# Blocks 1 to 7 of the first GEMM as seven half-size products, with a new mixing of the tiles

## The chip, the cores and the metric

One core of a Trainium2 chip runs the whole program. The metric is the device time in microseconds; the median of three runs stands for a kernel.

## What is computed

x is 4 x 1024 x 1024 (batch, time, channels), fside has the same shape, W1 is 4096 x 1024, W2 is 1024 x 4096. A two-sided decaying average over time mixes the tokens, then a feed-forward layer is added to x. Cut to what matters:

```python
def reference(x, fside, cond, w, u, W1, W2):
    r, k, v, time_emb = x, fside, fside, cond
    tf = sigmoid(sum(time_emb))
    decay = exp(-exp(w)) * (0.5 + 0.5 * tf)
    ek = exp(minimum(k, 30)); ekv = ek * v
    # nf, df: running sums of ekv, ek forward in time, each step times decay
    # nb, db: the same backward in time
    euk = exp(minimum(u + k, 30))
    num = nf + nb - ekv + euk * v
    den = df + db - ek + euk
    mixed = sigmoid(r) * (num / maximum(den, 1e-8)) * (0.8 + 0.2 * tf)
    h = einsum('bsd,fd->bsf', mixed, W1)
    a = gelu(clip(round(h / 0.1)) * 0.1)
    return x + einsum('bsf,df->bsd', a, W2)
```

The entries of W1 and W2 are 0 or a sign times a power of two from 1 to 1/16, so they are exact in float16.

## The kernel before

The work is cut into eight blocks: four batches times two halves of the time axis, 512 tokens each. Channels lie on the partitions, tokens on the free axis. A block has two parts on TensorE: the hidden stage (first GEMM, `hidden`, L378; for the first two steps of block 0 `first_hidden`, L364) and the output stage (`output`, L393). Both use float16 operands and split each activation in a high and a low half, so that each weight tile of 128x128 meets two matmuls of 512 columns. That makes 8 channel tiles x 32 feature tiles x 2 = 512 matmuls per stage and block. Each result of the hidden stage goes through a quantising copy to int16 (L495), gelu (L502), a scaled copy to float16 (the high half, L508), all on ScalarE, and the low half on VectorE (L805).

The operands of the first GEMM come from the mixing of tiles: a tile is 128 channels of a block. ScalarE takes exp of fside (L448, L450) and tanh of x (L455), VectorE does the forward and backward scans, the sums, a reciprocal (L780) and the gate, and the two halves go to `mix` (L488, L588), which has two slots, one for the block in use and one for the next. The second block of a batch in the order of work (the late half first, then the early one) takes the carry of the first; late tiles first scan the whole early half (`prefix`, L704 to L709) to know the state at the middle. Tiles of block 0 (`first_tile`, L620 to L684) take ln and exp on ScalarE (L482, L484) and a Newton step in place of the reciprocal. The mixing of block n+1 runs beside block n, four tiles in its hidden stage and four in its output stage.

Order on each engine is written out by hand; each queue runs in order. GpSimd casts W1 and W2 from float32 to float16 in DRAM while block 0 is mixed (L339, L341). SyncE (SP) issues all other DMAs: ring slots of 1 MB of weights (w_ring, 4 slots), tiles, residuals, stores. SP also loads 512 KB of the float32 weights and 256 KB of the float16 ones (L237, L238), eight pairs per block, and VectorE compares them (L819). If a comparison or a bound on fside fails, a general float32 path runs behind a flag; with the given inputs it does not.

```python
            def output(n, i, weights, parts, loaded, s_act, start):

                for k in range(2):
                    loaded(k)
                    pe.wait_ge(s_res[k], FREE + ITER * n + i)
...
                    if next_b is not None:
                        load_tile(CT * (n + 1) + i, CT * next_b + i, next_b, slot == 1, i)
```

Of the kernel before, what the change touches and what calls it, by code (L numbers as in the profile page):

```python
# [5 lines left out]
P = 128  # L20
# [3 lines left out]
F32 = mybir.dt.float32  # L24
I16 = mybir.dt.int16
# [7 lines left out]
OUT_SCALE = 64.0  # L33
ACT_SCALE = 16.0
FREE = 1
V_LIMIT = 1000.0


def adaln_ffn_kernel(nc, x, fside, cond, w, u, w1, w2, out):
# [7 lines left out]
    ITER = STEPS // 2  # L47
    CHUNK = FPS * CT * P
    PIECE = CHUNK // ITER
    assert DT == STEPS == CT and HALVES == 2 and FPS == 4 and CHUNK == FT * P  # L50

    with ExitStack() as ctx:
# [6 lines left out]

        w1_half = nc.dram_tensor("w1_half", [STEPS, P, CHUNK], F16).ap()  # L60
        w2_half = nc.dram_tensor("w2_half", [DT, P, CHUNK], F16).ap()
        w1_full = w1.rearrange("s p j c m -> s p (j c m)")
        w2_full = w2.rearrange("s p f m -> s p (f m)")


        w_ring = sb("w_ring", [P, 4, CHUNK], F16)
        act = sb("act", [P, FT, 2, T], F16)
        mix = sb("mix", [P, 2, CT, 2, T], F16)
        w1_ring = w_ring[:, 0:2, :].rearrange("p s (j c m) -> p s j c m", j=FPS, c=CT)
        w1_first = w_ring[:, 2:4, :].rearrange("p s (j c m) -> p s j c m", j=FPS, c=CT)  # L70
        w2_ring = w_ring[:, 2:4, :].rearrange("p s (f m) -> p s f m", f=FT)
# [3 lines left out]
        w2_gen = w_gen.rearrange("p s (f m) -> p s f m", f=FT)  # L75
        act_gen = act[:, :, :, :].bitcast(F32).rearrange("p f a t -> p f (a t)")
        mix_gen = mix[:, :, :, :, :].bitcast(F32).rearrange("p s c a t -> p s c (a t)")

        V = sb("V", [P, 2, T], F32)
        R = sb("R", [P, 2, T], F32)


# [5 lines left out]
        RCP = sb("RCP", [P, 2, T], F32)  # L90

        VP = sb("VP", [P, 2, T], F32)
        EKP = sb("EKP", [P, 2, T], F32)
        EKVP = sb("EKVP", [P, 2, T], F32)
        carry = sb("carry", [P, 2, CT], F32)

        q16 = sb("q16", [P, 2, T], I16)
        a32 = sb("a32", [P, 4, T], F32)
        xy = sb("xy", [P, 2, T], F32)
        chk_full = sb("chk_full", [P, PIECE], F32)  # L100
        chk_half = sb("chk_half", [P, PIECE], F16)

        w_sb = sb("w_sb", [P, CT], F32)
        u_sb = sb("u_sb", [P, CT], F32)
        cond_sb = sb("cond_sb", [P, B, TD], F32)
        tsum = sb("tsum", [P, B], F32)
        tf = sb("tf", [P, B], F32)
        dfac = sb("dfac", [P, B], F32)
        ogain = sb("ogain", [P, B], F32)
        ogain_gen = sb("ogain_gen", [P, B], F32)  # L110
        ogain_neg = sb("ogain_neg", [P, B], F32)
        decay = sb("decay", [P, B, CT], F32)
        bad = sb("bad", [P, BLOCKS * 2 * ITER], F32)
        vsum = sb("vsum", [P, BLOCKS * CT], F32)
# [4 lines left out]


        h_ps = [[ctx.enter_context(nc.psum_tensor(f"h_ps{k}{j}", [P, T], F32)) for j in range(FPS)] for k in range(2)]
        Y_AT = FPS - 2
        y_ps = h_ps[0][Y_AT:]
        f_ps = h_ps[0][0]

# [5 lines left out]
        s_w1cast0 = [sem(f"s_w1cast0_{k}") for k in range(4)]  # L131
        s_w1cast = sem("s_w1cast")
        s_w2cast = sem("s_w2cast")
# [3 lines left out]
        s_exps = sem("s_exps")  # L137
        s_expp = sem("s_expp")
        s_tanh = sem("s_tanh")
        s_ekp = sem("s_ekp")  # L140
        s_ekvp = sem("s_ekvp")
        s_denp = sem("s_denp")
        s_nump = sem("s_nump")
# [3 lines left out]
        s_vchk = sem("s_vchk")  # L147
        s_vsq = sem("s_vsq")
        s_vbon = sem("s_vbon")
# [3 lines left out]
        s_dbwd = sem("s_dbwd")  # L153
        s_carry = sem("s_carry")
        s_num1 = sem("s_num1")
        s_den1 = sem("s_den1")
        s_num2 = sem("s_num2")
        s_den2 = sem("s_den2")
        s_den3 = sem("s_den3")
        s_ln = sem("s_ln")  # L160
        s_rcp0 = sem("s_rcp0")
        s_newton = sem("s_newton")
        s_rcp = sem("s_rcp")
# [773 lines left out]
```

## Time and profile before

| | us |
|---|---|
| median of 3 runs (1900.64 to 1901.31) | 1900.69 |
| the profiled execution, its span | 1898.6 |
| TensorE busy with matmuls | 1788.5 |
| VectorE busy | 1342.6 |
| ScalarE busy | 735.2 |
| matmuls of the output stages (4096 at L393) | 885.4 |
| matmuls of the hidden stages (3968 at L378) | 860.8 |
| first matmuls of block 0 (128 at L364) | 44.8 |

Busy time is a union over instructions, and matmuls are pipelined, so their mean durations are longer than their distance in the stream. Distances are read from the chain of waits. The page has no time of the profiled execution besides its span.

### The profile page before, as it was taken

The page shows a single profiled execution, that of the slowest core. Times are in us where ns is not written, and L with a number is a line of the kernel's source. Part 1 is how long each engine was busy: PE and PEld are TensorE (multiplying, and loading weights), DVE is VectorE, ACT ScalarE, POOL GpSimd, SP SyncE. Part 2 cuts the span into 40 slices and gives each one's busy share as a digit, 9 for nine tenths or more (in the row PEclk, how much of TensorE's full clock was granted, in tenths as well). Part 3 has the DMA queues.
Part 4 walks back from the last instruction along what each step waited for, and adds up shares of the span by engine and source line. Part 5 has one row for each costly group of instructions (what it writes and reads, how often), then busy time and mean ns, then how long its engine had stood idle before and what let it go on. Part 6 is the DMA issues. An engine that isn't in the chain of part 4 may idle for free.

```text
span 1898.6 us, 24557 instructions
## 1 busy us (share of the span) xinstructions
PE 1788.5 (94%) x8194; PEld 805.5 (42%) x8194; DVE 1342.6 (71%) x1916; ACT 735.2 (39%) x1200; POOL 8.1 (0%) x20
## 2 busy tenths in 40 slices
PE   1358999999999999999999999999999999999998
PEld 0123444444444444444444444444444444444443
DVE  8986896698966796599986786588985777622111
ACT  4446611465116621366214641176313652034200
POOL 0000000000000000000000000000000000000000
PEclk9678999999999999999999999999999999999999
DMA  8585444434453344434443334534354334433133
GB/s 236 140 191 175 144 166 139 166 118 154 160 173 131 124 147 158 169 116 155 166 157 142 120 139 144 180 130 147 145 177 154 107 142 155 160 112 122 67 123 104
DMA packets 79576, 277.80 MB, mean 146 GB/s; under 512 B 9264, under 2 KB 9264, under 8 KB 62640
## 3 DMA queue, kind: packets, MB, share of 16 engines
q1 hardware_dynamic: 78768, 260.61, 39.3%
q0 software_dynamic: 768, 16.78, 4.3%
q14 instruction: 30, 0.25, 0.0%
q8 instruction: 10, 0.16, 0.0%
HBM read 277.36 MB, written 33.55 MB: 164 GB/s over the span
## 4 chain that ended last, share of the span: by engine, by line
PE 91%; DVE 5%; issue 2%; DMA 1%; ACT 0%; DVEq 0%; SPq 0%
PE h_ps L393 47%; PE h_ps L378 45%; DMA V<-in_fside_dram 1%; DVE DEN L636 1%; DVE EKP L633 0%; DVE NUM L660 0%; DVE NUM L681 0%; DVE DEN L664 0%; DVE EKV L630 0%; DVE DEN L670 0%; DVE V L667 0%; DVE EKVP L628 0%; DVE RCP L652 0%; DVE DEN L644 0%; DVE mix L588 0%
## 5 line engine op out<-in xcount | busy, mean ns | idle before, releaser
L393 PE MATMUL h_ps<-act,w_ring 128*128 128x512 f16 x4096 | 885.4, 379 | 0.0
L378 PE MATMUL h_ps<-mix,w_ring 128*128 128x512 f16 x3968 | 860.8, 380 | 8.6 <-ACT q L495 8.6
L393 PEld LDWEIGHTS h_ps<-act,w_ring 128*128 128x128 f16 x4096 | 400.8, 98 | 483.3
L378 PEld LDWEIGHTS h_ps<-mix,w_ring 128*128 128x128 f16 x3968 | 388.9, 98 | 479.2 <-ACT q L495 9.1
L805 DVE SCALAR_TENSOR_TENSOR act<-a,act 128x512 f32 (+1 forms) x256 | 164.9, 686 | 227.5 <-ACT act L508 227.3
L488 ACT ACTIVATE mix<-NUM 128x512 f32 (+1 forms) x64 | 40.1, 626 | 670.5 <-DVE NUM L783 623.9
L495 ACT ACTIVATE q<-h_ps 128x512 int16<-128x512 f32 x256 | 148.1, 591 | 333.2 <-PE h_ps L378 331.8
L812 DVE SCALAR_TENSOR_TENSOR xy<-h_ps,xy 128x512 f32<-128x512 f32 x64 | 43.9, 687 | 222.6 <-PE h_ps L393 222.6
L780 DVE RECIPROCAL DEN<-DEN 128x512 f32<-128x512 f32 x56 | 187.4, 3347 | 0.0
L502 ACT ACTIVATE a<-q 128x512 f32<-128x512 int16 x256 | 146.7, 622 | 0.6
L508 ACT ACTIVATE act<-a 128x512 f32 (+1 forms) x256 | 145.4, 617 | 0.0
L364 PE MATMUL h_ps<-mix,w_ring 128*128 128x512 f16 x128 | 44.8, 528 | 93.2 <-DVE mix L588 93.2
L819 DVE SCALAR_TENSOR_TENSOR chk_half<-chk_full,chk_half 128x1024 f16<-128x1024 f32 x64 | 77.9, 1217 | 0.0
L749 DVE TENSOR_TENSOR_SCAN EKV<-EKV,decay 128x512 f32<-128x512 f32 x56 | 71.9, 1284 | 2.8
L752 DVE TENSOR_TENSOR_SCAN EK<-EK,decay 128x512 f32<-128x512 f32 x56 | 70.5, 1259 | 0.0
L364 PEld LDWEIGHTS h_ps<-mix,w_ring 128*128 128x128 f16 x128 | 15.8, 129 | 121.6 <-DVE mix L588 61.0
L588 DVE TENSOR_TENSOR mix<-NUM,mix 128x512 f32 (+1 forms) x64 | 44.1, 689 | 28.4 <-ACT mix L488 28.4
L783 DVE SCALAR_TENSOR_TENSOR NUM<-NUM,ogain,DEN 128x512 f32<-128x512 f32 x56 | 42.1, 752 | 6.7 <-DVE DEN L780 0.6
L502 ACT ACT_TABLE_LOAD x36 | 46.2, 1283 | 0.6
L715 DVE TENSOR_SCALAR EK<-EK 128x512 f32<-128x512 f32 x56 | 23.2, 415 | 27.9 <-ACT EK L448 27.8
L448 ACT ACT_TABLE_LOAD x32 | 41.1, 1283 | 4.3 <-DMA V<-in_fside_dram 3.9
L730 DVE TENSOR_TENSOR_SCAN NUM<-decay,EKV 128x512 f32<-128x512 f32 x32 | 39.1, 1222 | 2.4 <-DVE EKV L721 0.6
(91 smaller groups left out, 903.7 us busy)
## 6 DMA issues: line engine op xcount, KB each, us to landing
w_ring<-w_half SPq DMA_DIRECT2D x128, 1024.0 KB, 4.9
chk_full<-in_w_dram SPq DMA_DIRECT2D x64, 512.0 KB, 5.7
V<-in_fside_dram SPq DMA_DIRECT2D x64, 256.0 KB, 4.3
R<-in_x_dram SPq DMA_DIRECT2D x64, 256.0 KB, 4.1
w_half<-in_w_dram POOLq DMA_DIRECT2D x16, 1024.0 KB, 11.4
xy<-in_x_dram SPq DMA_DIRECT2D x64, 256.0 KB, 2.7
chk_half<-w_half SPq DMA_DIRECT2D x64, 256.0 KB, 5.9
out_dram<-xy SPq DMA_DIRECT2D x64, 256.0 KB, 5.2
```

The lines of the kernel that those rows point to most:

```text
L364: mm = pe.matmul(h_ps[k][j][:, :], w1_first[:, k, j, c, :], mix[:, 0, c, p, :], start=(c == 0 and p == 0), stop=(c == CT - 1 and p == 1))
L378: mm = pe.matmul(h_ps[k][j][:, :], weights[:, k, j, c, :], rhs, start=(c == 0 and p == 0), stop=(c == CT - 1 and p == len(parts(c)) - 1))
L393: mm = pe.matmul(y_ps[k][:, :], weights[:, k, f, :], rhs, start=(f == 0 and p == 0), stop=(f == FT - 1 and p == len(parts(f)) - 1))
L495: nc.scalar.activation(q16[:, t % 2, :], h_ps[k][j][:, :], ACT.Copy, scale=scale).then_inc(s_q[k][j], 1)
L502: nc.scalar.activation(a32[:, j, :], q16[:, t % 2, :], ACT.Gelu_apprx_tanh, scale=QSTEP).then_inc(s_gelu[j], 1)
L508: nc.scalar.activation(act[:, 2 * FPS * i + t, 0, :], a32[:, j, :], ACT.Copy, scale=ACT_SCALE).then_inc(s_ahi[j], 1)
L588: v.tensor_tensor(mix[:, slot, c, 1, :], NUM[:, k, :], mix[:, slot, c, 0, :], ALU.subtract).then_inc(s_mix, 1)
L749: v.tensor_tensor_scan(EKV[:, 0, 0:T][:, ::-1], EKV[:, 0, 0:T][:, ::-1], dec(b, c), EKV[:, 0, T:T + 1], ALU.add, ALU.mult).then_inc(s_nbwd, 1)
L752: v.tensor_tensor_scan(EK[:, 0, 0:T][:, ::-1], EK[:, 0, 0:T][:, ::-1], dec(b, c), EK[:, 0, T:T + 1], ALU.add, ALU.mult).then_inc(s_dbwd, 1)
L780: v.reciprocal(DEN[:, 0, :], DEN[:, 0, :]).then_inc(s_rcp, 1)
L805: v.scalar_tensor_tensor(out=act[:, 2 * FPS * i + t, 1, :], in0=a32[:, j, :], scalar=ACT_SCALE, in1=act[:, 2 * FPS * i + t, 0, :], op0=ALU ...
L819: v.scalar_tensor_tensor(out=chk_half[:, :], in0=chk_full[:, :], scalar=1.0, in1=chk_half[:, :], op0=ALU.mult, op1=ALU.not_equal, accum_ou ...
```

## The change

`first_hidden` and the hidden stage of block 0 stay plain (512 matmuls of 512 columns). In blocks 1 to 7 the first GEMM of four feature tiles by eight channel tiles by 512 tokens is cut in halves in each of the three directions and done as seven products of half-size matrices (Winograd's form of Strassen's algorithm). A product is 2 feature tiles x 4 channel tile pairs x 2 halves = 16 matmuls of 256 columns. Seven operands, B11, B21, B22 and the sums T1 to T4, are kept in `mo`, high and low half each; they are made of pairs of mixed tiles, q = 0 to 3. `mo` has one slot, so the operands of block n+1 are written in the output stage of block n (`operand_sums`, `operands_hi`, `operands_lo`), the last pair after the last tile. Sums of weights are made on VectorE in block 0 (`weight_sums`) and stored in DRAM; GpSimd copies the three plain quarters. The products chain in PSUM: ScalarE copies P1 to a second bank (`seed`) and P5 to SBUF (`spill_p5`), VectorE adds P5 to form U4 (`seed_u4`) and C22 (`quantise22`).

The ring has eight slots of 512 KB, and its loads follow one list; each waits until the entry eight places ahead is used. The checks convert on ScalarE (`check_i8`) instead of loading the float16 copy, and lie in the output stage, one per output tile, except the first. All tiles are mixed as those of block 0 were, with ln, exp and one Newton step; ln and exp share an activation table there. The prefix of a late tile is no longer scanned: VectorE adds a ramp times ln(decay) to fside, ScalarE takes exp with its sum, VectorE takes the dot product with its sum. Activations are handled two feature tiles (1024 elements) at a time. All loops are unrolled.

```diff
-            def hidden(n, i, weights, parts, loaded):
-
-                pe.wait_ge(s_mix, FREE + CT * (n + 1))
...
+            def product(dst, k, r, op, fresh, need=None):
+                for f in range(2):
+                    for q in range(KH):
+                        if need is not None and f == 0:
+                            pe.wait_ge(s_mo, need(q))
+                        for p in range(2):
+                            mm = pe.matmul(dst[:, f, :], wp_ring[:, k, r, f, q, :], mo[:, op, q, p, :],
+                                           start=(fresh and f == 0 and q == 0 and p == 0),
+                                           stop=(q == KH - 1 and p == 1), skip_group_check=True)
+                return mm
...
+                    for s in range(STEPS):
+                        products_15(n, s)
+                        if s > 0:
+                            products_73(n, s - 1)
+                        products_26(n, s)
+                        if s > 0:
+                            product_4(n, s - 1)
+                output(n, 0, 0)
+                if n > 0:
+                    products_73(n, LAST)
+                output(n, 1, 0)
+                if n > 0:
+                    product_4(n, LAST)
+                output(n, 0, 1)
+                output(n, 1, 1)
...
+                load_check(DT * n + 1)
+                for d in range(2, DT):
+                    ring_load()
+                    store(n, d - 2)
+                    residual(n, d)
+                    ring_load()
+                    if nxt and d in (2, 4):
+                        load_tile(g0 + 5 + d // 2)
+                    if d == 6 and n + 2 < BLOCKS:
+                        load_tile(g0 + CT)
+                    load_check(DT * n + d)
...
+                if nxt:
+                    divide(g0 + 7)
+                check(at + 7)
+                if nxt:
+                    operand_sums(n + 1, 3)
+                    operands_lo(n + 1, 3)
+                residual_sum(n, 7)
...
+            def hidden_block(n, nxt, g0):
+                for s in range(STEPS):
+                    if s >= 2:
+                        quantise21(n, s - 2)
+                        gelu(n, s - 2, 1)
+                    seed(n, s)
+                    if s >= 2:
+                        act_hi(n, s - 2, 1)
+                    spill_p5(n, s)
+                    if nxt and s % 2 == 0:
+                        tile_group(g0 + s // 2)
+                    if s >= 1:
+                        quantise12(n, s - 1)
+                        gelu(n, s - 1, 0)
+                    quantise11(n, s)
+                    if s >= 1:
+                        act_hi(n, s - 1, 0)
...
+                for s in range(STEPS):
...
+                    act_lo(0, s, 0)
+                    weight_sums(2 * s)
+                    weight_sums(2 * s + 1)
```

SP's queue at the end of the output stage of block 0, before: s_y is raised by TensorE once per output tile, s_res by the residual sum on VectorE.

```order
L290 DMA w_ring<-w_half 128x4096 [waits s_y]
L263 DMA out_dram<-xy 128x512 [waits s_res1]
L259 DMA xy<-in_x_dram 128x512 [waits s_store1]
L290 DMA w_ring<-w_half 128x4096 [waits s_y]
L237 DMA chk_full<-in_w_dram 128x1024 [waits s_chk]
L238 DMA chk_half<-w_half 128x1024
L263 DMA out_dram<-xy 128x512 [waits s_res0]
L290 DMA w_ring<-w_half 128x4096 [waits s_y]
L263 DMA out_dram<-xy 128x512 [waits s_res1]
```

The same place after the change, from the release of the slot of output tile 6 to the first release by a product (s_p5). A slot of w_ring is now 128x2048.

```order
L303 DMA w_ring<-w1s 128x1024 [waits s_y]
L310 DMA VP<-in_fside_dram 128x512 [waits s_dot]
L317 DMA V<-in_fside_dram 128x512 [waits s_gate]
L318 DMA R<-in_x_dram 128x512
L335 DMA chk_full<-in_w_dram 128x1024 [waits s_chk]
L303 DMA w_ring<-w1s 128x2048 [waits s_y]
L329 DMA out_dram<-xy 128x512 [waits s_res1]
L324 DMA xy<-in_x_dram 128x512 [waits s_store1]
L303 DMA w_ring<-w1s 128x2048 [waits s_y]
L335 DMA chk_full<-in_w_dram 128x1024 [waits s_chk]
L303 DMA w_ring<-w1s 128x2048 [waits s_p5]
```

The check's load used to be issued behind the release by output tile 6; the last one now stands behind the release by output tile 7, the last of the stage.

VectorE's queue there, before: the end of the turn of the output stage that mixes a tile (L775 to L588, whose result waits in a slot of mix), residual sums (L812) and the check (L819).

```order
L775 SCALAR_TENSOR_TENSOR NUM<-R,NUM 128x512 [waits s_tanh,s_num2]
L780 RECIPROCAL DEN<-DEN 128x512 [waits s_den3]
L783 SCALAR_TENSOR_TENSOR NUM<-NUM,ogain,DEN 128x512 [waits s_rcp,s_gate]
L588 ISA [waits s_mixhi]
L588 REGISTER_ALU
L588 TENSOR_TENSOR mix<-NUM,mix 128x512
L810 REGISTER_ALU
L812 SCALAR_TENSOR_TENSOR xy<-h_ps,xy 128x512 [waits s_x1,s_y]
L818 REGISTER_ALU
L819 REGISTER_ALU [waits s_chkload]
L819 SCALAR_TENSOR_TENSOR chk_half,bad<-chk_full,chk_half 128x1024
```

After, from the residual sum of tile 6 to that of tile 7. L932 to L942 divide the last tile, L1107 is the check, L1039 to L1043 are the operand sums of the last pair (a is their scratch), L1049 to L1054 write its low halves to mo.

```order
L1099 SCALAR_TENSOR_TENSOR xy<-ps,xy 128x512 [waits s_x0,s_y]
L932 TENSOR_TENSOR DEN<-DEN,RCP 128x512 [waits s_rcp0]
L935 SCALAR_TENSOR_TENSOR RCP<-DEN,RCP 128x512 [waits s_newton]
L942 SCALAR_TENSOR_TENSOR m_st<-NUM,ogain_neg,RCP 128x512 [waits s_gate,s_newton]
L1107 SCALAR_TENSOR_TENSOR chk_full,bad<-chk_i,chk_full 128x1024 [waits s_chki8]
L1039 TENSOR_TENSOR a<-m_st 128x512 [waits s_out]
L1041 TENSOR_TENSOR a<-m_st,a 128x256 [waits s_t]
L1043 TENSOR_TENSOR a<-m_st,a 128x256 [waits s_t]
L1049 TENSOR_TENSOR mo<-m_st,mo 128x256 [waits s_mohi]
L1051 TENSOR_TENSOR mo<-m_st,mo 128x2x256 [waits s_mohi]
L1054 TENSOR_TENSOR mo<-a,mo 128x4x256 [waits s_mohi]
L1099 SCALAR_TENSOR_TENSOR xy<-ps,xy 128x512 [waits s_x1,s_y]
```

The check came last and nothing followed from it; now it stands ahead of the last operands of the next block.

## Rows read from the trace of the kernel before

**Rows 1.** The page, parts 1 (busy us, share, instructions) and 2 (clock in tenths).
```profile
PE 1788.5 (94%) x8194; PEld 805.5 (42%) x8194; DVE 1342.6 (71%) x1916; ACT 735.2 (39%) x1200; POOL 8.1 (0%) x20
...
PEclk9678999999999999999999999999999999999999
```

**Rows 2.** The chain of waits in order of time: start us, us, what.
```profile
130.46 20.64 DMA V<-in_fside_dram
...
153.42 79.06 PE h_ps L378 x352
232.48 110.51 PE h_ps L393 x512
342.99 110.51 PE h_ps L378 x512
...
1779.57 110.52 PE h_ps L393 x512
```

**Rows 3.** VectorE's timeline, tiles 7 and 8: start us, us, line, operation.
```profile
103.02 1.26 DVE L636 TENSOR_TENSOR_SCAN DEN<-decay,EKP,EK 128x512 f32<-128x512 f32 x1
...
114.43 0.42 DVE L620 TENSOR_SCALAR EKP<-EKP 128x512 f32<-128x512 f32 x1
...
115.10 0.68 DVE L628 TENSOR_TENSOR EKVP<-EKP,VP 128x512 f32<-128x512 f32 x1
...
116.31 1.22 DVE L633 TENSOR_TENSOR_SCAN EKP<-decay,EKP 128x512 f32<-128x512 f32 x1
117.44 1.20 DVE L634 TENSOR_TENSOR_SCAN EKVP<-decay,EKVP 128x512 f32<-128x512 f32 x1
118.56 1.26 DVE L636 TENSOR_TENSOR_SCAN DEN<-decay,EKP,EK 128x512 f32<-128x512 f32 x1
...
133.56 0.69 DVE L588 TENSOR_TENSOR mix<-NUM,mix 128x512 f16<-128x512 f32 x1 [0.70 <-ACT mix L488]
```

**Rows 4.** TensorE's timeline around its pause, [idle before <-releaser].
```profile
128.72 5.25 PE L364 MATMUL h_ps<-mix,w_ring 128*128 128x512 f16 x16 [9.35 <-DVE mix L588]
...
137.77 7.07 PE L378 MATMUL h_ps<-mix,w_ring 128*128 128x512 f16 x32
153.42 11.94 PE L378 MATMUL h_ps<-mix,w_ring 128*128 128x512 f16 x41 [8.58 <-ACT q L495]
```

**Rows 5.** Landing times of the casts of w2 (L341), then the checks (L237).
```profile
L341 POOL DMA_DIRECT2D w_half<-in_w_dram x8: 491/491/493, 103.0 to 106.4; - x8
...
DMA to landing us min/median/max: 11.8/28.2/44.1
...
DMA to landing us min/median/max: 3.8/5.7/7.7
```

**Rows 6.** Busy us by window, the granted clock, DMA share and GB/s last.
```profile
110.00:120.00 10.00, 6.19 (x16) 2.14 (x16) 9.90 (x18) 4.14 (x5) 0.00 (x0) 0.58 0.97 208
150.00:160.00 10.00, 6.58 (x17) 2.39 (x18) 4.86 (x8) 8.85 (x16) 0.00 (x0) 0.53 0.85 325
```

**Rows 7.** Groups by line and shape: xcount | busy us, mean ns | idle before.
```profile
L393 PEld LDWEIGHTS h_ps<-act,w_ring 128*128 128x128 f16 x4096 | 400.8, 98 | 483.3
...
L495 ACT ACTIVATE q<-h_ps 128x512 int16<-128x512 f32 x256 | 148.1, 591 | 333.2 <-PE h_ps L378 331.8 <-PE h_ps L364 1.4
...
L805 DVE SCALAR_TENSOR_TENSOR act<-a,act 128x512 f32 x192 | 123.7, 686 | 131.9 <-ACT act L508 131.7 <-issue 0.2
...
L819 DVE SCALAR_TENSOR_TENSOR chk_half<-chk_full,chk_half 128x1024 f16<-128x1024 f32 x64 | 77.9, 1217 | 0.0
...
L502 ACT ACT_TABLE_LOAD x36 | 46.2, 1283 | 0.6
```

**Rows 8.** SyncE's queue at a stage's start: start us, us, what is issued.
```profile
688.35 0.34 SPq L290 DMA_DIRECT2D w_ring<-w_half  x1
688.79 0.38 SPq L237 DMA_DIRECT2D chk_full<-in_w_dram  x1
```

**Rows 9.** The page, part 6: DMA issues, KB each, median us to landing.
```profile
w_ring<-w_half SPq DMA_DIRECT2D x128, 1024.0 KB, 4.9
```

More of the change, by code:

```diff
@@ L24 @@
 F32 = mybir.dt.float32
+I8 = mybir.dt.int8
 I16 = mybir.dt.int16
@@ L366, in first_hidden @@
-                            if c == CT - 1:
-                                mm.then_inc(s_h, 1)
-            def hidden(n, i, weights, parts, loaded):
-                pe.wait_ge(s_mix, FREE + CT * (n + 1))
-                for k in range(2):
-                    loaded(k)
+                                mm = pe.matmul(bank[4 * s + j][:, :], w1_ring[:, slots[2 * s + j // 2], j % 2, c, :],
+                                               mix0[:, c, p, :], start=(t == 0 and p == 0), stop=(t == CT - 1 and p == 1))
@@ L398, in ffn_block @@
-            def ffn_block(n, b, next_b, slot):
-                first = isinstance(n, int) and n == 0
-                if first:
-                    first_hidden()
-                with pe.Fori(int(first), ITER) as i:
-                    hidden(n, i, w1_ring, lambda c: [mix[:, slot, c, p, :] for p in range(2)],
-                           lambda k: pe.wait_ge(s_w1[k], 16 * (ITER * n + i + 1)))
-                with pe.Fori(0, ITER) as i:
-                    output(n, i, w2_ring, lambda f: [act[:, f, p, :] for p in range(2)],
-                           lambda k: pe.wait_ge(s_w2[k], 16 * (ITER * n + i + 1)), s_alo, FREE)
@@ new lines, in _, with hidden_block0 @@
+            exps(0, 0)
+            tanh(0)
+            for t in range(CT):
+                if t + 1 < CT:
+                    exps(t + 1, t)
+                if t > 0:
+                    mix_hi(t - 1)
+                reciprocal(t)
+                if t + 1 < CT:
+                    tanh(t + 1)
+            mix_hi(CT - 1)
+            def hidden_block0(g0):
+                for s in range(STEPS):
+                    quantise0(s, 0)
+                    quantise0(s, 1)
+                    gelu(0, s, 0)
+                    quantise0(s, 2)
+                    quantise0(s, 3)
+                    act_hi(0, s, 0)
+                    gelu(0, s, 1)
+                    act_hi(0, s, 1)
+                    if s % 2 == 0:
+                        tile_group(g0 + s // 2)
+                tile_group(g0 + 4)
@@ new lines, in general_block @@
+            def general_block(m):
+                n = BLOCKS + m
+                for t in range(CT):
+                    g = CT * n + t
+                    exps(g, g)
+                    reciprocal(g)
+                    tanh(g)
+                for s in range(STEPS):
+                    for j in range(FPS):
+                        f = FPS * s + j
+                        act_e.wait_ge(g_h, FT * m + f + 1)
+                        sc.activation(q16[:, s % 2, j, :], bank[4 * (s % 2) + j][:, :], ACT.Copy,
+                                      scale=1.0 / QSTEP).then_inc(g_q, 1)
+                        act_e.wait_ge(g_q, FT * m + f + 1)
+                        if m > 0 and f == 0:
+                            act_e.wait_ge(g_y, DT * m)
+                        sc.activation(act_gen[:, f, :], q16[:, s % 2, j, :], ACT.Gelu_apprx_tanh,
+                                      scale=QSTEP).then_inc(g_gelu, 1)
@@ L895, in _ @@
             with dve.If(needs_general > 0):
-                each_block(dve, general_block, BLOCKS)
+                for m in range(BLOCKS):
+                    general_block(m)
 def kernel(**inputs):
```

1407 lines of the change are left out of this document (854 added, 553 removed).

## The prediction

> **What bounds the kernel now.** I read the busy times first: the matmuls fill 94% of the span [rows 1]. Then the chain of waits in order of time: after 153.42 us it is matmuls alone, in stages of 512 matmuls that take 110.51 us each, without a gap, whichever GEMM it is [rows 2]. So one matmul of 512 columns costs 110.51 / 512 = 215.8 ns in the stream, and 512 / 2.4 GHz = 213.3 ns of it is array time; the granted clock is full, 9 tenths or more in each slice from there on [rows 1]. Everything after 153 us is bound by TensorE; nothing else is paid for there. Ahead of it the mixing of the first eight tiles on VectorE sets the pace (one tile per 15.54 us, from one scan of DEN to the next [rows 3]). Between them is one pause of 8.58 us of TensorE. ScalarE ends it, held in its queue behind a load of V that took 20.64 us to land [rows 2, 4], because the casts of the weights, issued from 103 us on, occupied the DMA engines (their landing times go up to 44.1 us [rows 5]). The 41 matmuls after the pause take 11.94 us instead of 41 x 0.2158 = 8.85 us: a pause of this length is followed by 3.09 us of loss; the clock granted around it is 0.53, near the 1.2 GHz level [rows 4, 6].
>
> I set the profiled execution (span 1898.6 us) against the change. The median of the runs is 1900.7 us, 2.1 us above it, and I add these 2.1 us at the end. About 0.2% (3.8 us) is what a measurement can tell from no change.
>
> **Term 1, the products.** Blocks 1 to 7 replace 512 matmuls of 512 columns by 8 x 7 x 16 = 896 of 256 columns. If the 2.5 ns above array time stay per instruction, one costs 106.7 + 2.5 = 109.2 ns. Were all of it to scale, 107.9 ns. I take 109.2, as the 2.5 ns look fixed: 97.8 us per block, 12.7 us less, seven times: **-88.8 us**. Each keeps its weight load; a load lasts 98 ns [rows 7], which fits under 109 ns but no longer with the room it had under 216. The Trainium skill, in "TensorE: Matmul & The Clock Gate", section Back-to-back issue gap, speaks against this term: it has pairs of load and matmul at about 81 ns for 128 columns, 25 ns above the matmul alone. An estimate from that page, the same 25 ns on each of 6272 short matmuls, would add 157 us; nothing of it shows in the rows of 512 columns.
>
> **Term 2, the hand-over from an output stage to the next block.** This decides. Before, the operands of the next block wait in mix, complete, and the weight checks sit where nobody waits for them. After, SP issues the load of a block's last check only behind its wait for the release of the ring slot of output tile 7, so after the last matmul E of the output stage. VectorE has that check ahead of the operand sums of the last pair of tiles in its queue, and the first matmul product needs that pair (its fourth wait on s_mo). The path, from E:
> - ring load, then the check's load. In the trace 1 MB of ring, then 512 KB of check are issued 0.44 us apart [rows 8], the check lands 5.7 us after its own issue (3.8 to 7.7) [rows 5], a ring load 4.9 us after its own [rows 9]. From the difference some 0.37 MB per us. The ring part is now 512 KB: landed at E + 5.0 (bounds 4.3 and 6.2).
> - ScalarE's conversion to int8, 1024 elements: VectorE takes 1217 ns for 1024 where it takes 686 ns for 512 [rows 7]; ScalarE's 591 ns for 512 become 1.05 us by the same ratio: E + 6.2.
> - the check on VectorE, 1.2 us [rows 7]: E + 7.4. Three dependent operand sums of 512, 256 and 256 elements, 0.77 + 0.5 + 0.35 us of queue, and the subtraction that ends B11, 0.4 us: E + 9.4.
> The operands of T1 follow at E + 11.4, through one conversion and one 1024-element subtraction; the cold matmuls before them hide this. TensorE can do the six matmuls of the first three pairs at once (0.65 us), then it stands until E + 9.4: 8.75 us idle, about the pause seen at 144.84 us. So 3.1 us of low clock follow: 11.9 us per hand-over. There are seven: **+83 us**. Bounds: 9 us (early landing, clock back sooner) to 14 us, so +63 to +98 us. The check before it, and the reciprocal of the last tile with its two table loads of 1.28 us [rows 7], run by E + 4.3 and are covered by this one. The residual sum of tile 7 and its store move 12 us later and nobody waits. In the last block SP's ring loads are used up, its checks run ahead, and the tail stays as it is.
>
> **Term 3, the start.** Per tile VectorE loses a min (0.34 us of queue), a product (0.60) and two scans (1.13 and 1.12) [rows 3] and gains ramp x ln(decay), the sum with V, the weighted product with its accumulator, and two memsets (0.34 + 0.70 + 0.68 + 0.12), and EKV now waits 0.08 us for EK just ahead of it: 15.54 becomes 14.27 us. Seven periods save 8.9 us; the logarithm of the decay ahead of the first tile costs 0.5 us; the last tile's operand, now begun at 133.56 us [rows 3], is 8.8 us earlier (0.4 us of it since ln and exp come to share a table). ScalarE, busy 4.14 of 10 us there [rows 6], covers its added work. But then TensorE pauses again: the casts still hold the DMA engines until about 148 us, and R of tile 8 lands behind V of tile 8 (issued near 108 us; such loads took some 20 us each among the casts). Its tanh stands before the quantising in ScalarE's queue, so hidden step 3 begins near 150 us instead of 144.6. Then the weight sums, 8 VectorE instructions per step of block 0 (0.42 to 0.69 us each [rows 3, 7]), wait for loads that SP issues only after the sums before them. They delay the lower activation parts, then the gelus, then the quantising: I count 2.5 us of stall. End of block 0: near 336 us instead of 342.99, **-7 us** (bounds -15 and +15).
>
> **Term 4, stalls inside the product stages.** A pair of steps has 24.4 us of TensorE. ScalarE has nine PSUM, gelu and split instructions per step and a tile group with three table loads every second: 22 us. VectorE has half a tile per step, two splits and two PSUM sums: 22 to 23 us. Walked through in queue order, ScalarE's split of step s-1 in an even step ends at 15.6 us, VectorE then needs 19.1 us of queue until it delivers C22 of the odd step; TensorE wants it 19.4 us after, so 0.3 us are spare where the next tiles are late ones (with prefix) and 1.4 us otherwise. In the output stage the residual sum of tile 2 comes within 0.2 us of when TensorE wants its bank back. I take 1 us per block, **+7 us** (0 to 25). The ring's 1.75 MB per step are no bound: slots are refilled two steps ahead, and SP's other waits are over when it reaches them.
>
> **Sum:** 1898.6 - 88.8 + 83 - 7 + 7 = 1892.8, with 2.1 us: **1895 us**. The saving in the products is given back at the hand-overs; what is left is the start.
>
> **Rivals.**
> - A, the hand-over costs little: part of the check's path is hidden, or the loads land earlier than I hold, and 7 x 10 us come back: 1825 us. For it: the products do save 89 us. Against: each link is in program order, and the shortest landing (3.8 us) still gives 8 us of pause. Chance 0.10.
> - B, ScalarE and VectorE become the bound in the products (slower than before). Their loop has 0.3 us to spare in 24; each further us per pair of steps costs 4 us per block. If the PSUM-to-PSUM copy, the int16 outputs or the 1024-element activations take 5% more than their nearest rows, the loop is 1.2 us longer: +4 us per block over my sum, +28 us: 1923 us. It decides from 0.6 us more per loop on (+9 us, 1904). For: the narrow margins. Against: the rows include such PSUM reads at no extra cost. Chance 0.17.
> - C, the weight load shows under the short matmul: if a quarter of its 98 ns does, 24.5 ns x 6272 = +154 us: 2049 us. For: it has 11 ns of room. Against: no row shows a matmul waiting for a load. This is what the Trainium skill's figure above would mean. Chance 0.04.
> - D, block 0 is held up by its loads: copies and sums add about 20 MB of traffic right after the casts. If every second step waits 6 us more, +24 us: 1919 us. Chance 0.07.
>
> **How the numbers follow.** My forecast has 0.62; the bounds put it within 15 us either side of 1895, so of it 0.35 lies faster by over 0.2%, 0.12 within, 0.15 slower. A is faster (0.10); B (0.17), C (0.04) and D (0.07) are slower, but 0.03 of B and D, at a part of their price, falls within 0.2%. Together 0.45, 0.15 and 0.40. Cases of both signs hold much of the chance; the likeliest one's own range is 1880 to 1912. The range for 8 in 10 takes in B and D and the low end of term 2: 1866 to 1932. A beyond it and C are left out.
>
> **What would show it.** Right: between the last matmul on act and the steady stream on mo, seven pauses of TensorE of 8 to 10 us after six short matmuls, ended by VectorE's subtraction that writes mo, the last check's load issued some 0.5 us after E, and a low clock after it. Short matmuls at 109 ns apart; stages of products of 98 us plus pause; the last operand of block 0 near 125.5 us; a pause near 145 us ended by ScalarE. Wrong: no idle at the start of blocks (A), pauses inside the stages ended by the seeds of U4 or C22 (B), spacing near 130 ns (C), a block 0 ending after 345 us (D).

## The result, and the profile after

| | before | after |
|---|---|---|
| median of the runs, us | 1900.7 (1899.5 to 1901.3, 4 runs) | 1909.85 (1906.45 to 1911.78, 4 runs) |
| ratio, 95% interval | 1 | 1.0047 (1.0033 to 1.0061) |
| span of the profiled execution, us | 1898.6 | 1904.6 |

The change makes the kernel 0.5% slower. The 1895 us forecast had the wrong sign; the measured time lies inside the range. The page of the kernel after, parts 1, 2 and 5, which answers to [rows 1]:

```profile
span 1904.6 us, 27493 instructions
PE 1723.3 (90%) x10882; PEld 1076.1 (57%) x10882; DVE 1281.7 (67%) x2040; ACT 1046.7 (55%) x1422; POOL 24.7 (1%) x44
PE   1367989899998999899998999989998999989998
PEclk9678999899998999999998999989998999999999
L561 PE MATMUL ps<-act,w_ring 128*128 128x512 f16 x4096 | 890.1, 379 | 9.4 <-DVE xy L1099 9.4
L505 PE MATMUL ps<-mo,w_ring 128*128 128x256 f16 x6272 | 704.4, 276 | 61.2 <-DVE mo L1049 59.6
```

TensorE's share fell to 90%, and its line and that of the clock now dip all along the blocks, where they were flat. The dips are waits of 59.6 us in all for DVE's subtraction L1049, one per block. TensorE's timeline (start us, us, what, [idle before <-releaser]) shows the start, block 0 and three hand-overs (a hand-over is the passage from the output stage of one block to the products of the next); it answers to [rows 2] and [rows 4]:

```profile
132.25 13.98 PE L495 MATMUL ps<-mo,w_ring 128*128 128x512 f16 x64
153.82 16.32 PE L495 MATMUL ps<-mo,w_ring 128*128 128x512 f16 x64 [7.59 <-ACT q L699]
170.70 7.07 PE L495 MATMUL ps<-mo,w_ring 128*128 128x512 f16 x32 [0.56 <-ACT q L699]
181.84 8.77 PE L495 MATMUL ps<-mo,w_ring 128*128 128x512 f16 x32 [4.07 <-DMA w_ring<-w_half]
194.91 43.89 PE L495 MATMUL ps<-mo,w_ring 128*128 128x512 f16 x192 [4.30 <-ACT q L699]
238.63 27.79 PE L561 MATMUL ps<-act,w_ring 128*128 128x512 f16 x128
271.90 29.14 PE L561 MATMUL ps<-act,w_ring 128*128 128x512 f16 x128 [5.48 <-DVE xy L1099]
301.30 55.41 PE L561 MATMUL ps<-act,w_ring 128*128 128x512 f16 x256 [0.26 <-DVE xy L1099]
357.61 0.82 PE L505 MATMUL ps<-mo,w_ring 128*128 128x256 f16 x6 [0.90 <-DVE xy L1099]
366.00 94.14 PE L505 MATMUL ps<-mo,w_ring 128*128 128x256 f16 x842 [7.58 <-DVE mo L1049]
...
521.47 55.41 PE L561 MATMUL ps<-act,w_ring 128*128 128x512 f16 x256 [0.84 <-DVE xy L1099]
576.82 0.81 PE L505 MATMUL ps<-mo,w_ring 128*128 128x256 f16 x6
586.26 94.92 PE L505 MATMUL ps<-mo,w_ring 128*128 128x256 f16 x842 [8.63 <-DVE mo L1049]
...
1237.90 0.81 PE L505 MATMUL ps<-mo,w_ring 128*128 128x256 f16 x6 [0.35 <-DVE xy L1099]
1247.64 93.66 PE L505 MATMUL ps<-mo,w_ring 128*128 128x256 f16 x842 [8.92 <-DVE mo L1049]
```

Block 0 ends at 356.7 us (301.30 + 55.4), where it ended at 342.99 before [rows 2]. The last block ends at 1897.4, so a block takes 1540.7 / 7 = 220.1 us; before it took 221.02, two stages of 110.51 [rows 2]. The account of the span, 6.0 us longer: block 0 +13.7, seven blocks -6.4, the tail behind the last matmul 7.2 instead of 8.5 us.

One hand-over, read from four queues (block 4 to 5, last matmul E at 1237.5 us). SyncE, ScalarE, VectorE, from their timelines:

```profile
1237.59 0.32 SPq L303 DMA_DIRECT2D w_ring<-w1s  x1
1237.95 0.43 SPq L335 DMA_DIRECT2D chk_full<-in_w_dram  x1
...
1243.40 1.06 ACT L758 ACTIVATE chk_i<-chk_full 128x1024 int8<-128x1024 f32 x1 [3.72 <-DMA chk_full<-in_w_dram]
...
1244.48 1.23 DVE L1107 SCALAR_TENSOR_TENSOR chk_full<-chk_i,chk_full 128x1024 f32<-128x1024 int8 x1 [2.57 <-ACT chk_i L758]
...
1245.63 0.69 DVE L1039 TENSOR_TENSOR a<-m_st 128x512 f32<-128x512 f32 x1
1246.36 0.42 DVE L1041 TENSOR_TENSOR a<-m_st,a 128x256 f32<-128x256 f32 x1
1246.82 0.43 DVE L1043 TENSOR_TENSOR a<-m_st,a 128x256 f32<-128x256 f32 x1
1247.16 0.42 DVE L1049 TENSOR_TENSOR mo<-m_st,mo 128x256 f16<-128x256 f32 x1
```

The check lands at E + 5.9, is converted by E + 7.0 and done by E + 8.1, and L1049 ends at E + 10.1; the prediction had 5.0, 6.2, 7.4 and 9.4.

Block 0 is late for another reason. ScalarE, SyncE and VectorE in the hidden stage of block 0:

```profile
146.38 0.63 ACT L649 ACTIVATE EK<-V 128x512 f32<-128x512 f32 x1 [8.24 <-DMA V<-in_fside_dram]
```
```profile
129.92 8.14 SPq L303 DMA_DIRECT2D w_ring<-w_half  x1
...
169.63 3.41 SPq L303 DMA_DIRECT2D w_ring<-w_half  x2
```
```profile
160.41 0.42 DVE L1062 TENSOR_TENSOR mo<-mo 128x512 f16<-128x512 f16 x1 [24.35 <-DMA mo<-w_half]
...
178.08 0.43 DVE L1062 TENSOR_TENSOR mo<-mo 128x512 f16<-128x512 f16 x1 [6.76 <-DMA mo<-w_half]
...
271.07 0.68 DVE L1099 SCALAR_TENSOR_TENSOR xy<-ps,xy 128x512 f32<-128x512 f32 x1
```

VectorE stands 24.35 and 6.76 us on the first loads of the weight sums (L1062). From 182 us on it is busy without a gap over 1 us, and its backlog still makes residual sum 0 (L1099) come at 271.07 us, when TensorE has waited 5.48 us for it. The wait of 4.07 us on the weight ring has its root in the same sums: SyncE's queue waits for VectorE before it stores a sum, 33.2 us in four waits between 120 and 200 us, and the ring load that TensorE needs at 181.84 us stands behind such a store and is issued at 169.63 us only. After 153.82 us, 832 matmuls would take 179.5 us at 215.8 ns each and end at 333.4 us; the 23.3 us more are 14.7 us of idle in five waits and 8.6 us of slower matmuls behind them.

The traffic between 95 and 145 us, from the view of the DMA queues (KB each, median us to landing):

```profile
w_half<-in_w_dram POOLq DMA_DIRECT2D x9, 1024.0 KB, 31.3
w1s<-w_half POOLq DMA_DIRECT2D x24, 256.0 KB, 53.6
w_ring<-w_half SPq DMA_DIRECT2D x5, 512.0 KB, 20.0
V<-in_fside_dram SPq DMA_DIRECT2D x2, 256.0 KB, 34.9
R<-in_x_dram SPq DMA_DIRECT2D x2, 256.0 KB, 38.6
mo<-w_half SPq DMA_DIRECT2D x2, 256.0 KB, 35.3
sp<-w_half SPq DMA_DIRECT2D x2, 256.0 KB, 38.0
```

### The profile page after: what moved, and what is told of

Same layout as the page of the kernel before. It is cut to its first block, busy times and chain, and to the rows that moved or that the text cites. A ratio compares the mean times of both kernels' runs of the same rounds, so it can differ in the third digit from the quotient of the medians.

```text
span 1904.6 us, 27493 instructions
## 1 busy us (share of the span) xinstructions
PE 1723.3 (90%) x10882; PEld 1076.1 (57%) x10882; DVE 1281.7 (67%) x2040; ACT 1046.7 (55%) x1422; POOL 24.7 (1%) x44
## 4 chain that ended last, share of the span: by engine, by line
PE 79%; DMA 3%; DVE 3%; ACT 1%; issue 1%; SPq 0%; DVEq 0%
PE ps L561 42%; PE ps L505 37%; DMA chk_full<-in_w_dram 3%; DVE chk_full L1107 1%; ACT chk_i L758 1%; DVE a L1039 0%; ACT mo L695 0%; DVE a L1041 0%; DVE a L1043 0%; DVE xy L1099 0%; SPq L303 0%; SPq L317 0%; DVE mo L1049 0%; SPq L318 0%; ACT q L699 0%
## 5 line engine op out<-in xcount | busy, mean ns | idle before, releaser
L561 PE MATMUL ps<-act,w_ring 128*128 128x512 f16 x4096 | 890.1, 379 | 9.4 <-DVE xy L1099 9.4
L505 PE MATMUL ps<-mo,w_ring 128*128 128x256 f16 x6272 | 704.4, 276 | 61.2 <-DVE mo L1049 59.6
L505 PEld LDWEIGHTS ps<-mo,w_ring 128*128 128x128 f16 x6272 | 620.5, 99 | 146.7 <-DVE mo L1049 61.6
L561 PEld LDWEIGHTS ps<-act,w_ring 128*128 128x128 f16 x4096 | 400.6, 98 | 490.9 <-issue 15.5
L758 ACT ACTIVATE chk_i<-chk_full 128x1024 int8<-128x1024 f32 x64 | 67.5, 1054 | 440.3 <-DMA chk_full<-in_w_dram 440.3
L1107 DVE SCALAR_TENSOR_TENSOR chk_full<-chk_i,chk_full 128x1024 f32<-128x1024 int8 x64 | 78.3, 1223 | 252.5 <-ACT chk_i L758 252.3
L1092 DVE SCALAR_TENSOR_TENSOR act<-a,act 128x1024 f16<-128x1024 f32 x128 | 156.2, 1220 | 132.3 <-ACT act L751 132.3
L745 ACT ACTIVATE a<-q 128x1024 f32<-128x1024 int16 x128 | 135.3, 1057 | 31.4 <-DVE act L1092 27.2
L751 ACT ACTIVATE act<-a 128x1024 f16<-128x1024 f32 x128 | 134.2, 1049 | 0.9
L482 PE MATMUL ps<-mo,w_ring 128*128 128x512 f16 x128 | 45.1, 532 | 87.3 <-DVE mo L1032 87.3
L495 PE MATMUL ps<-mo,w_ring 128*128 128x512 f16 x384 | 90.0, 399 | 16.5 <-ACT q L699 12.5
L482 PEld LDWEIGHTS ps<-mo,w_ring 128*128 128x128 f16 x128 | 16.1, 130 | 115.8 <-issue 58.6
L729 ACT ACTIVATE q<-ps 128x512 int16<-128x512 f32 x56 | 33.2, 594 | 85.6 <-PE ps L505 85.6
L495 PEld LDWEIGHTS ps<-mo,w_ring 128*128 128x128 f16 x384 | 38.8, 102 | 67.5 <-issue 22.1
L1099 DVE SCALAR_TENSOR_TENSOR xy<-ps,xy 128x512 f32<-128x512 f32 x64 | 43.8, 685 | 30.8 <-PE ps L561 30.8
```

Of the source, the lines that this page charges most:

```text
L495: mm = pe.matmul(bank[4 * (s % 2) + j][:, :], w1_ring[:, k, f, c, :], mix0[:, c, p, :], start=(c == 0 and p == 0), stop=(c == CT - 1 and p ...
L505: mm = pe.matmul(dst[:, f, :], wp_ring[:, k, r, f, q, :], mo[:, op, q, p, :], start=(fresh and f == 0 and q == 0 and p == 0), stop=(q == K ...
L561: mm = pe.matmul(y_ps[y][:, :], w2_ring[:, k, f, :], act[:, a, p, :], start=(a == 0 and p == 0), stop=(a == FT - 1 and p == 1))
L745: sc.activation(a32[:, 2 * h:2 * h + 2, :], q16[:, s % 2, 2 * h:2 * h + 2, :], ACT.Gelu_apprx_tanh, scale=QSTEP).then_inc(s_gelu, 1)
L751: sc.activation(act[:, f:f + 2, 0, :], a32[:, 2 * h:2 * h + 2, :], ACT.Copy, scale=ACT_SCALE).then_inc(s_ahi, 1)
L758: sc.activation(chk_i8[:, :], chk_full[:, :], ACT.Copy, scale=W_SCALE).then_inc(s_chki8, 1)
```

## Experiments on the hand-over

All are edits of the changed kernel (1909.85 us), each timed against the kernel before.

**Check's load first** (SyncE's queue alone; the line issues the loads of checks 2 to 7 of every output stage):

```diff
 for d in range(2, DT):
+    load_check(DT * n + d)
     ring_load()
     store(n, d - 2)
...
-    load_check(DT * n + d)
```

> Edit: only SyncE's queue; in the output stage the load of check d is issued at the head of iteration d, ahead of the stage's weight loads, store, residual and tile loads. Theory 1 (the path last matmul E, issue of the last check's load at E + 0.4, landing, conversion, check, sums): the last load leaves about 10 us earlier, at the end of check 6, lands before E, and the divide of the last tile ends near E; the seven pauses of 7.6 to 8.9 us ahead of L505 (59.6 us in all) fall to 0 to 2 us each, and the change gains 45 to 60 us: near 1855 us. Rival 1 (the pause is the divide's: Ln and Exp with two table loads, reciprocal and the sums come too late anyway, at E + 4.4 in the trace): at least 5 us of each pause stay, and the gain is 27 us or less: 1883 us or more.

Measured: 1825.6 us (1824.3 to 1827.9), ratio to before 0.9607 (0.9591 to 0.9623): 84 us less than the change, more than the 45 to 60 I had expected from the idle alone. TensorE's timeline of this kernel:

```profile
357.58 92.74 PE L505 MATMUL ps<-mo,w_ring 128*128 128x256 f16 x848
450.15 7.07 PE L561 MATMUL ps<-act,w_ring 128*128 128x512 f16 x32
...
469.21 96.86 PE L561 MATMUL ps<-act,w_ring 128*128 128x512 f16 x448
565.90 92.74 PE L505 MATMUL ps<-mo,w_ring 128*128 128x256 f16 x848
```

From 357.58 us to the last matmul of the output stages there is no row with an idle time. A block now takes 565.90 - 357.58 = 208.32 us, against 220.1: 11.8 us per hand-over, 82.5 in all. Of it 8.7 us are the pause with the six matmuls less what those take in the stream, 2.2 us the slow matmuls behind it (842 take 94.25 us on the mean, and 842 of the 848 here 92.1), and 0.7 us the small waits for L1099 at output tile 4 and ahead of the first product, which went too; some 0.2 us stay without a row. I had left the last two out of the expectation, though the prediction counted the slow matmuls.

**Engines' order** (VectorE's and ScalarE's queues alone):

```diff
 residual_sum(n, 6)
 if nxt:
     divide(g0 + 7)
-check(at + 7)
 if nxt:
     operand_sums(n + 1, 3)
     operands_lo(n + 1, 3)
 residual_sum(n, 7)
+check(at + 7)
```

and ScalarE's check_i8(at + 7) behind operands_hi(n + 1, 3).

> Edit: only VectorE's and ScalarE's order at the end of a block; the last pair's sums and roundings stand ahead of the last check and its conversion, and SyncE's queue is as in the change. Theory 1: PE then waits for the divide alone, which ended 4.4 us after E (1241.9 us against 1237.5 us): sums 1.3 us and B11's low part 0.4 us behind it, so the pause ahead of L505 is near 5 us where it was 8.9, and the gain is 7 times 3.5 to 4.5 us: 1878 to 1886 us. Rival 1 (the last check's load was in the way of the divide as well, by the DMA or by ScalarE): no gain beyond 10 us. Rival 2 (the wait just moves to spills behind the check): a pause of 3 us or more appears at the second or third product of each block, and less than half of the gain is seen.

Measured: 1884.7 us, ratio 0.9911 (0.9895 to 0.9928), 25 us less. The pause at block 5:

```profile
1233.78 26.46 PE L505 MATMUL ps<-mo,w_ring 128*128 128x256 f16 x225 [5.13 <-DVE mo L1049]
```

This is what was expected (1878 to 1886 us). So two paths end near each other: the check's at E + 10, the divide's at E + 6. The second exists only because the check before the last is late as well: its load stands behind a ring load too, and the divide behind it. In the change that check is converted at E - 6.7 and the last tile's divide ends at E + 4.4; with the check's load first they come at E - 21.4 and E - 7.1.

**Both.**

> Edit: both of the above. Theory 1: pauses ahead of L505 fall to 0 to 1 us, 1845 to 1855 us, within 5 us of the first edit alone, since either path then ends near E. If the two gains add up (about 27 plus 55 us), the theory of one path is wrong.

Measured: 1826.4 us (1825.3 to 1827.2). This is below the expected 1845 to 1855 us, as the first edit alone was below its own, but within 1 us of that edit: the gains are not additive, and with the load first the engines' order costs nothing. The cause of the seven pauses is the place of the checks' loads, one line, in SyncE's queue. How much the last of the six loads does alone was not tried; the run before shows that the one before it counts as well.

## Experiments on block 0

**Copies late** (GpSimd waits for s_h0 >= 16 before its 24 copies):

> Edit: only GpSimd's queue; the 24 copies of weights into the table of products are issued behind a wait until PE has done hidden step 3 of block 0, instead of right behind the casts. Theory 2 (block 0 is late by 14 us because casts and copies hold the DMA from 103 to 200 us, so that the loads of the weight sums take 35 us to land and VectorE stands 24 us on them): the loads issued at 123 us land 10 to 20 us earlier, VectorE's wait is 5 to 15 us, and the end of block 0 moves from 356.7 to 340 to 347 us: 1893 to 1900 us. Rival (the weight sums' own arithmetic on VectorE, 0.42 us each, and their order ahead of the activations set the end of block 0): the wait may shrink, and the end stays within 4 us of 356.7, the time within 5 us of 1909.9.

Measured: 1909.3 us; no difference. VectorE's first wait shrank from 24.35 to 18.56 us, the hidden stage ended 5 us sooner (233.4 us), but another wait of 8.42 us on a sum's load came at 194 us, and the residual sum came at the same 271 us. In all VectorE stood 34.9 us on loads of the sums, against 34.1 us in the change. The copies were not what held V: it landed at 145.7 us, against 146.4. The rival was right about the time; the next run tests its mechanism.

**Sums two hidden steps later** (stores, loads and arithmetic, in two queues):

```diff
-                    weight_sums(2 * s)
-                    weight_sums(2 * s + 1)
+                    if s >= 2:
+                        weight_sums(2 * s - 4)
+                        weight_sums(2 * s - 3)
```

> Edit: only the weight sums of block 0: their stores, loads and arithmetic stand two hidden steps later in SyncE's and VectorE's queues, with the last four behind the stage; the same work, the same DMAs. Theory 3 (block 0 is late since VectorE stands 24 + 2 + 7 + 1 us on loads of the sums at 134 to 181 us, and the backlog reaches residual sum 0 at 271 us): the waits go, PE no longer waits at 194.91 (4.30 us) and 271.90 (5.48 us), nor runs slowly behind them; the end of block 0 comes at 341 to 346 us where it was 356.7, and the time is 1895 to 1900 us. Rival (VectorE's arithmetic alone, 16 times 1.6 us of sums, fills block 0): the residual sum still comes near 271 us, and the time is 1906 us or more. In both the first pause of 7.6 us, on the mixing tile whose V lands at 146 us, stays.

Measured: 1901.4 us (10 runs, 1898.2 to 1902.5), 8.5 us less by the medians and 5.4 by the spans. TensorE's timeline:

```profile
153.62 70.90 PE L499 MATMUL ps<-mo,w_ring 128*128 128x512 f16 x320 [7.88 <-ACT q L703]
224.35 27.79 PE L565 MATMUL ps<-act,w_ring 128*128 128x512 f16 x128
264.13 30.51 PE L565 MATMUL ps<-act,w_ring 128*128 128x512 f16 x128 [11.99 <-DVE xy L1103]
```

The hidden stage ends 14.3 us sooner, but 6.5 us of it are lost again in the output stage, where the pause grows from 5.48 to 11.99 us, and block 0 ends at 350.9 us, 5.8 us sooner. The time lies between the two expectations, since each was half right: the waits on the sums in their old place cost the hidden stage 14 us, and VectorE's backlog, in which the sums' arithmetic still stands, holds residual sum 0 until 263 us.

**Casts of w2 late** (GpSimd waits for s_mix >= 8 before them, and for the end of the hidden stage before the copies):

> Edit: only GpSimd's queue: the casts of the second weights wait for the last operand of block 0 (about 127 us), and the copies into the table of products wait for the end of the hidden stage. Theory 4 (the casts of the second weights hold the DMA from 100 to 145 us, so that V of the first overlapped tile lands at 146 us and the first sums at 160 us): V lands before 130 us and ScalarE doesn't wait for it, the first sums land by 150 us, the stall of 7.59 us ahead of hidden step 2 falls below 3 us, VectorE's wait on the sums below 15 us, and the end of block 0 comes at 332 to 345 us: 1885 to 1898 us. Rival (the traffic only moves: 25 MB of casts take their 45 us wherever they stand, and the second loads of the sums and the weight ring wait in turn): the first stall goes, others of the same sum come at 150 to 200 us, the end of block 0 stays above 350 us, and the time is 1903 us or more.

Measured: 1918.5 us, ratio 1.0088 (1.0072 to 1.0105), 8.6 us more. TensorE's timeline:

```profile
133.15 34.70 PE L497 MATMUL ps<-mo,w_ring 128*128 128x512 f16 x160
180.24 8.87 PE L497 MATMUL ps<-mo,w_ring 128*128 128x512 f16 x32 [12.40 <-DMA w_ring<-w_half]
...
265.37 9.83 PE L563 MATMUL ps<-act,w_ring 128*128 128x512 f16 x36 [8.90 <-DVE act L1094]
```

The pause at 146 us is gone, so the casts were its cause; 12.4 us on the weight ring and 8.9 us more came for it, as the rival had it. The first of them comes through SyncE's queue: its two issues of a sum's load at 140.45 us took 29.64 us, and the ring load stood behind them. In this kernel the traffic that has to be done before the output stage gained nothing from being put later.

**Check's load first, and casts late.**

> Edit: the check's load at the head of each iteration (which gave 84 us) together with the edit on GpSimd's queue. If block 0 and the hand-overs are independent, the time is 1825.6 us less what the edit on GpSimd's queue gives by itself, to within 3 us.

Measured: 1835.0 us, 9.4 us more than the check's load first alone, where the casts late had cost 8.6 us by themselves: the two parts are independent within 1 us.

**The same, and the sums later.**

> Edit: as the one before, with the weight sums two hidden steps later as well. Theory 3 with theory 4: VectorE waits for no sum, and the end of block 0 is set by PE's own work from 131 us on (384 + 512 matmuls at 0.219 us are 196 us, and at most two short stalls): 330 to 336 us, 1800 to 1806 us. Rival: if VectorE's arithmetic sets block 0, this is within 3 us of the one before.

Measured: 1829.7 us. Outside both expectations; pauses of 12.7 and 17.7 us stood in the output stage, since the copies, now issued at the end of the hidden stage, delayed the last sums and V of a tile by 10 and 14 us. A bad place for the copies.

**Residual sums 0 and 1 early** (on top of the check's load first; casts and copies as in the change):

```diff
                 part(0, g0 + 4)
+                residual_sum(0, 0)
                 part(1, g0 + 4)
+                residual_sum(0, 1)
                 part(2, g0 + 4)
```

> Edit: the check's load at the head of each iteration, and in block 0 the residual sums 0 and 1 ahead on VectorE, between the parts of the fifth overlapped tile (same work). Theory 5 (after the hidden stage PE waits for a residual sum that stands behind VectorE's backlog: 6.91 us ahead of 272.63 us): residual sum 0 runs near 260 us, the pause is under 1 us, and the end of block 0 comes 5 to 8 us before the 357.0 us of the first edit: 1817 to 1821 us. Rival (another step of the output stage is as late: the check, its load or the weight ring): no more than 2 us are won.

Measured: 1816.8 us, 8.8 us less; block 0 ends at 350.7, its output stage without a pause.

**That, and the sums later.**

> Edit: as the one before, with the weight sums of block 0 two hidden steps later as well. Theory 3 with theory 5: PE's hidden stage of block 0 ends near 224 us as in the run with the sums alone, output sums 0 and 1 pass without a pause, and the end of block 0 comes at 336 to 339 us: 1803 to 1808 us. Rival (VectorE's arithmetic is the bound by itself, so the wait for a residual sum only moves): a pause of 5 us or more stays ahead of the third output tile, and the time is 1812 us or more.

Measured: 1810.5 us, 6.3 us less again. Block 0 ends at 341.7; the hidden stage ends at 223.4, and a pause of 5.05 us stands ahead of the fifth output tile, which waits for residual sum 2. Between the two expectations.

**That, and the casts in pairs**, each cast of w2 right behind that of w1 with its number:

```diff
                 pool.dma_start(w1_half[s], w1_full[s]).then_inc(s_w1cast[s], 16)
-            for d in range(DT):
-                pool.dma_start(w2_half[d], w2_full[d]).then_inc(s_w2cast[d], 16)
+                pool.dma_start(w2_half[s], w2_full[s]).then_inc(s_w2cast[s], 16)
```

> Edit: as the one before, and each cast of second weights is issued right behind the cast of first weights of the same number, so that the casts run beside the mixing from 20 to 110 us, where the DMA is busy under half of the time, and not behind it. Theory 4 in its other form (the traffic has to go where the DMA is idle): V of the first overlapped tile lands before 130 us, the pause of 7.9 us ahead of hidden step 2 goes, and 5 to 10 us more are won: 1795 to 1802 us. Rival (the loads of the mixing tiles are starved in turn): the tiles' period grows beyond 14.5 us, the last operand comes later than 127 us, and the time is that of the one before or longer.

Measured: 1802.8 us, 7.7 us less, 0.8 us above the expected range. By windows (busy us of PE, PEld, DVE, ACT, POOL, then clock, DMA share, GB/s), first the run before this one, then this one:

```profile
40.00:100.00 60.00, 24.60 (x75) 8.69 (x73) 58.89 (x106) 29.33 (x48) 3.83 (x8) 0.69 0.55 129
130.00:160.00 30.00, 24.08 (x106) 10.45 (x104) 8.41 (x11) 20.20 (x27) 0.00 (x0) 0.89 0.95 262
```
```profile
40.00:100.00 60.00, 24.68 (x69) 8.63 (x70) 58.75 (x106) 31.44 (x51) 4.07 (x8) 0.71 0.91 210
130.00:160.00 30.00, 30.00 (x141) 13.62 (x140) 16.10 (x22) 27.83 (x36) 0.00 (x0) 1.00 0.66 252
```

The casts moved into 40 to 100 us, where the DMA share went from 0.55 to 0.91, and left 130 to 160 us, where TensorE is now busy all the time. The loads of V issued between 95 and 145 us land after 8.4 us at the median instead of 34.9 us in the change, those of the sums after 12.2 and 15.2 instead of 35.3 and 38.0. The mixing paid 2.5 us for it, not in its period but once (the last 32 matmuls of the first hidden steps begin at 125.77 us instead of 123.29).

**The third residual sum early**, and on SyncE the store of output tile 0 and residual 2 ahead of the check's load, in block 0.

> Edit: all edits of the run before, and in block 0 the third residual sum stands ahead of the third check on VectorE, with the store of output tile 0 and the load of residual 2 ahead of that check's load on SyncE. Theory 5, once more: the last pause of block 0 (4.76 us ahead of 277.78 us, with 2.8 us of slow matmuls behind it) goes, PE works without a pause from 134.7 us to the last matmul, and the end of block 0 comes near 329 us: 1794 to 1797 us. Rival (residual 3 or a weight load is the next to be late): a pause of 2 us or more appears later in the output stage, and under 3 us are won.

Measured: 1800.65 us (1799.5 to 1801.8, 5 runs), ratio to before 0.9477 (0.9464 to 0.9489). Only 2 us less, as the rival had it:

```profile
216.37 69.23 PE L568 MATMUL ps<-act,w_ring 128*128 128x512 f16 x320
288.87 43.08 PE L568 MATMUL ps<-act,w_ring 128*128 128x512 f16 x192 [3.27 <-DVE xy L1106]
331.79 92.74 PE L512 MATMUL ps<-mo,w_ring 128*128 128x256 f16 x848
```

The pause moved on to residual sum 3. This version does the same computation as the change and is 5.2% faster than the kernel before.

## Why the prediction failed, step by step

- **Term 1 held to 0.1 us.** The period without pauses is 208.32 us where it was 221.02: -12.70 us per block, -88.9 against the predicted -88.8. 848 short matmuls and the start of the next group lie 92.57 us apart (357.58 to 450.15), 109.2 ns each, as predicted. Rival C is out: the 98 ns load is hidden under 109 ns. The Trainium skill's figure in "TensorE: Matmul & The Clock Gate", section Back-to-back issue gap (for 128 columns, 25 ns above the matmul alone), does not carry over to these 256 columns: the excess over array time (106.7 ns) is 2.5 ns.
- **Term 2 held in its mechanism and cost 76 us, not 83.** A pause costs 8.7 us, as counted, and the slow matmuls behind it 2.2 us on the mean where the prediction had 3.1: 10.8 us per hand-over instead of 11.9. The mechanism is shown: one line moved, and all seven pauses went. What was short in it: the check landed 0.9 us later than held, and the divide, which I had ended at E + 4.3, is a second path only 4 us shorter than the first.
- **Term 4 held in size, not in place.** The 82.5 us of the run with the check's load first leave 6 to 7 us beside Term 2, against 7. But no pause stands inside a product stage. What shows are waits for residual sums (L1099): 0.77 to 1.12 us at output tile 4, the place named there as within 0.2 us, in four of the seven blocks, and 0.28 to 0.90 us ahead of the first product in three hand-overs. They went with the check's load first, so they belong to the same cause. With it rival B is out.
- **Term 3 failed, and with it the sign.** Its first half held in the main: tiles come 14.46 us apart (predicted 14.27), the last operand is begun at 126.31 us, 7.3 us earlier than before (predicted 8.8; ln and exp of the last tile still load a table each), and hidden step 2 of block 0 begins at 132.25 us, 5.5 us earlier [rows 4]. The pause foreseen there came, and hidden step 3 began at 153.82 us, 3.8 us after the predicted 150. But "I count 2.5 us of stall" for the weight sums was wrong. From 150 us on the prediction left 6.5 us for stalls and slow matmuls; the trace has 23.3 us of them behind the start of that step. Block 0 ended at 356.7 us, not 336, 13.7 us later than before where 7 us earlier was forecast, at the far end of the bounds (+15). I priced the sums by their arithmetic and took their loads to land in the time of a quiet queue, though I had rows with landings of 28 to 44 us for the casts themselves [rows 5] and had held 20 us for V and R of the same moment. V, R and the sums' loads took 35 to 39 us; VectorE stood on them in order, with activation parts, a tile and residual sums queued behind. The residual sums early, the sums later and the casts in pairs (8.8, 6.3 and 7.7 us by the medians) bring the end of block 0 to 335.9 us. That this is the predicted figure is chance: it was forecast for the order of the change.
- **Rival D was the case**, with 0.07. Its place was right for the loads of the sums and wrong for the copies, which made no difference to the time when they were put later; the casts counted instead (7.7 us when put earlier). Its price (24 us) is close to the 20.7 us by which Term 3 missed, by luck, as its form was not right, since the stalls come from one load of V, two long waits of VectorE with SyncE's ring loads behind them, and VectorE's backlog, not from every second step.
- Summed: Term 3 +20.7 us, Terms 2 and 4 -7.6, the tail -1.3 make the span 11.8 us longer than the 1892.8 predicted. Another 3 us lie between the profiled execution, the fastest of four, and the median.

Open is how much of the arithmetic of the sums could be hidden at all; a kernel without them wasn't tried. Open too is why single DMA issues on SyncE took 8.14 and 29.64 us for two; no run separates the causes.

## What to carry to other kernels

When a change makes an engine's queue a link between two stages, follow every queue it passes to the place of the DMA issue: a load issued one wait too late cost this kernel 84 us, nearly all of the 89 us that the new algorithm saved, and one moved line gave it back. Work added under a stage that was hidden has to be priced with the landing times of that moment, not with quiet ones, and with everything behind it in its engine's queue. Move bulk traffic to where the DMA share is low: here that gained 7.7 us, while the same casts put later cost 8.6 us, since they met the next loads.

## What the runs showed of the hardware

- A matmul of 256 columns with its own weight load streams at 109.2 ns (the run with the check's load first) although the load alone is 98 ns long.
- Loads of 256 KB issued by SyncE while GpSimd's casts and copies were in flight took 35 to 39 us to land (4.5 us is the median of V's loads over the whole kernel), and one of SyncE's issues itself lasted 8.14 us, where the one at 1237.59 us lasted 0.32 us. With the copies put later V landed no sooner; with the casts of w2 put later its pause went.
- The slow matmuls behind a pause of 8.5 us cost 2.2 us on the mean (1.4 to 2.8), less than the 3.1 us after the pause of 8.58 us ahead of matmuls of 512 columns in the kernel before. The clock granted from 1247 to 1252 us, right behind one of these pauses, was 0.61 of 2.4 GHz.
